# Attention kernel: the weighting of the values moved to another place in the step, on TensorE, ScalarE and VectorE

## The reference, cut to what matters

```python
# query = layernorm(x), key = value = ctx, 32 query heads, 8 key/value heads, head size 128
q = (query @ wq)   # 1024 x 4096
k = (key @ wk)     # 1024 x 1024, each head used by 4 query heads
v = (value @ wv)   # 1024 x 1024
q, k = rope(q), rope(k)
raw = einsum('bhqd,bhkd->bhqk', q, k) / sqrt(128)
attn = softmax(raw + mask, axis=-1)
out = einsum('bhqk,bhkd->bhqd', attn, v)
x = x + tanh(g) * (out.reshape(1024, 4096) @ wo)
```

## Time and profile before

| | |
|---|---|
| median of three executions | 804.2 us |
| the profiled execution | 806.3 us, of which span 804.5 us |
| TensorE (PE) busy | 762.8 us, 95% of the span |
| VectorE (DVE) busy | 640.2 us, 80% |
| ScalarE (ACT) busy | 352.2 us, 44% |
| GpSimd (POOL) busy | 388.6 us, 48% |
| mean granted TensorE clock | 0.984 |

### The profile page before, as it was taken

The page is one execution under the profiler, slowest core; times in us unless marked ns, Lnnn a source line. Parts: engine busy times, 40 slices in busy tenths (PEclk is TensorE's granted clock), DMA queues, the critical chain, the costliest instruction groups (busy, mean ns, idle before and its releaser), DMA issues.

```text
span 804.5 us, 12801 instructions
## 1 busy us (share of the span) xinstructions
PE 762.8 (95%) x4278; PEld 607.7 (76%) x4278; DVE 640.2 (80%) x1209; ACT 352.2 (44%) x1077; POOL 388.6 (48%) x352
## 2 busy tenths in 40 slices
PE   3899998898989999999999999999999999999996
PEld 2576675887767778888878888877888888787875
DVE  5999997879888787767878777787877778868985
ACT  2878884412333423343342334334333433344664
POOL 2889986415553533323353333335333333386784
PEclk9899999998999999999999999999999999999998
DMA  8310140100021111011111100111110012210011
GB/s 258 104 53 26 33 124 2 40 28 25 29 63 42 52 39 42 26 32 40 35 46 38 51 27 27 40 40 41 39 54 27 27 34 85 56 30 1 2 40 66
DMA packets 37463, 37.45 MB, mean 47 GB/s; under 512 B 2912, under 2 KB 27232, under 8 KB 37408
## 3 DMA queue, kind: packets, MB, share of 16 engines
q1 hardware_dynamic: 35488, 33.20, 13.8%
q10 hardware_dynamic: 1920, 3.54, 1.4%
HBM read 34.64 MB, written 2.10 MB: 46 GB/s over the span
## 4 chain that ended last, share of the span: by engine, by line
PE 62%; DVE 8%; POOL 5%; issue 2%; ACT 1%; POOLq 0%; DVEq 0%; ACTq 0%
PE ROW L2080 6%; PE QB L2082 6%; PE QB L2080 6%; PE QB L2081 6%; PE SB L2195 6%; PE ROW L2081 6%; PE ROW L2082 6%; PE PB L2168 4%; DVE rope_b L1695 2%; PE KV L719 2%; PE KV L2080 2%; PE TB L2138 2%; PE KV L2082 1%; PE KV L2081 1%; PE KV L720 1%
## 5 line engine op out<-in xcount | busy, mean ns | idle before, releaser
L1260 POOL TENSOR_TENSOR dense<-rope_a,rope_b 128x512 f32<-128x512 f32 x62 | 79.2, 1278 | 163.8 <-DVE rope_b L1695 163.8
L1474 ACT ACTIVATE ot_hi<-PB 128x512 fp32r<-128x512 f32 x64 | 38.3, 598 | 199.2 <-PE PB L2168 199.1
L1463 ACT ACTIVATE e_sb<-masked,nmax 128x64 f32<-128x64 f32 x256 | 86.1, 337 | 57.0 <-DVE nmax L1726 56.7
L2080 PE MATMUL QB<-xT_hi,wq_lo 128*128 128x512 f32 x256 | 106.9, 417 | 0.0
L2080 PE MATMUL ROW<-wo_hi,ot_lo 128*128 128x512 f32 x256 | 102.1, 399 | 0.8 <-DVE ot_lo L1754 0.8
L2082 PE MATMUL QB<-xT_hi,wq_hi 128*128 128x512 f32 x256 | 101.7, 397 | 0.0
L2081 PE MATMUL QB<-xT_lo,wq_hi 128*128 128x512 f32 x256 | 101.6, 397 | 0.0
L1692 DVE TENSOR_TENSOR rope_a<-QB,rope 128x512 f32<-128x512 f32 x62 | 42.8, 691 | 73.9 <-PE QB L2082 71.8
L2081 PE MATMUL ROW<-wo_lo,ot_hi 128*128 128x512 f32 x256 | 101.6, 397 | 0.0
L2082 PE MATMUL ROW<-wo_hi,ot_hi 128*128 128x512 f32 x256 | 101.1, 395 | 0.0
L1695 DVE TENSOR_TENSOR rope_b<-QB,rope 64x512 f32<-64x512 f32 x124 | 85.4, 688 | 3.9
(11 more groups left out here) (215 smaller groups left out, 1883.4 us busy)
## 6 DMA issues: line engine op xcount, KB each, us to landing
raw<-in_wq SPq DMA_DIRECT2D x32, 256.0 KB, 2.7
raw<-in_wo SPq DMA_DIRECT2D x32, 256.0 KB, 2.6
ctx_two<-in_ctx SPq DMA_DIRECT2D x16, 256.0 KB, 3.8
x_sb<-in_x SPq DMA_DIRECT2D x8, 256.0 KB, 6.8
ctx_raw<-in_ctxT ACTq DMA_DIRECT2D x1, 2048.0 KB, 12.6
raw<-in_wv SPq DMA_DIRECT2D x8, 256.0 KB, 2.7
raw<-in_wk SPq DMA_DIRECT2D x8, 256.0 KB, 2.8
out<-x_sb SPq DMA_DIRECT2D x8, 256.0 KB, 2.0
```

The costliest lines, as they stand in the source:

```text
L1260: nc.gpsimd.tensor_tensor(dst, a, b, ALU.add).then_inc(s_rot, 1)
L1463: nc.scalar.activation(e_sb[:, r, :], masked[:, r, :], ACT.Exp, bias=nmax[:, r:r + 1], accum_out=zsum[:, r:r + 1]).then_inc(s_exp, 1)
L1474: nc.scalar.activation(ot_hi[:, :, :].rearrange("p h (b q) -> p b h q", b=2), PB2[:, :, 0:256].rearrange("p b (h q) -> p b h q", h=GH), AC ...
L2080: nc.tensor.matmul(out, lhs[1], rhs[0], start=first, stop=False)
```

## The change

Two small rules are added. `behind_transposes(n)` holds for n % 4 = 0, 1, 2. `at_the_end(gp, n)` holds for n % 4 = 2 and for the last step before the fourth pair. In a step of the first kind, TensorE now issues `weighted(N-2)` between the transposes and the query; in one of the second kind, it issues `weighted(N-1)` at the old place. So n % 4 = 0 and 1 have one block, early; n % 4 = 2 has two, one early and one late; n % 4 = 3 has none. ScalarE and VectorE follow: where the block is early, ScalarE rounds `pt` (now behind a wait for that block), then `ot`, and then takes the exponentials, and VectorE takes both low parts first, then makes the probabilities, then rotates the query. The fourth pair is not changed.

```diff
+        def behind_transposes(n):
+            return n % 4 < 3
+        def at_the_end(gp, n):
+            return n % 4 == 2 or (gp, n) == (LAST - 1, SLOTS - 1)
 # ScalarE, pair()
                     if N >= 1:
+                        if N >= 2:
+                            act.wait_ge(s_pv, N - 1)
                         round_pt(N - 1)
+                    if N >= 2 and behind_transposes(n):
+                        round_ot(N - 2)
                     exps(N)
-                    if N >= 1:
+                    if at_the_end(gp, n):
                         round_ot(N - 1)
 # VectorE, pair()
-                    if N == 0:
+                    if N >= 2 and behind_transposes(n):
+                        rest_ot(N - 2)
+                    first = N == 0 or N >= 2 and behind_transposes(n)
+                    if first:
                         normalize(N)
                     if n < 12 or ahead:
                         rope_q(q_job(gp, n), N + 4, n % 4)
-                    if N:
+                    if not first:
                         normalize(N)
                     if N >= 2:
                         accumulate(N - 2, (n - 2) % 8)
-                    if N >= 1:
+                    if at_the_end(gp, n):
                         rest_ot(N - 1)
 # TensorE, pair()
                     if N >= 1:
                         transposes(N - 1)
+                    if N >= 2 and behind_transposes(n):
+                        weighted(N - 2)
...
                     if N >= 2:
                         outputs(N - 2)
-                    if N >= 1:
+                    if at_the_end(gp, n):
                         weighted(N - 1)
```

## The result

Over 14 executions each, the median is 808.8 us with the change and 804.7 us without. The ratio is 1.0050, 95% interval 1.0039 to 1.0061, so the loss is small but clear of the noise. The profiled execution took 809.42 us with a span of 807.6; before it was 806.3 with 804.5. The forecast of +3.4 us stands against +4.1 in the medians and +3.1 in the spans.

What follows compares the result with a forecast made beforehand. TensorE, busy for 95% of the span, was taken to bound the kernel. Borders 2.96, start 0.74 and neutral blocks -0.3 summed to +3.4 us: 807.6 us on the 804.2 median. Its own range was 805.2 to 810, the wider one 803.0 to 811.5.

Steps and rivals of the forecast that it cites:

- A covered block: Block lying beside a TensorE wait at the old place; moved onto TensorE's path it adds 0.74 us.
- five places: Borders at steps 4, 8, 24, 40, plus the start: +0.74 us each where a wait had covered the block.
- the start: Step 1's block, ahead of the 2.33 us wait for `p_sb`, comes behind it: +0.74 us, out of 0.7 to 1.1.
- four borders: Steps 4, 8, 24, 40, where TensorE waits for a rotated query: 4 x 0.74 = 2.96 us lost.
- The price of a block on the path: Last pair, last transpose to second matmul behind the block: 0.97 us against 0.23 without, so 0.74 us.
- The neutral blocks: The 29 early blocks where TensorE doesn't wait: -0.01 us each from a cheaper entry, -0.3 in all.
- `ot_lo` in time behind a key projection: Eleven n % 4 = 2 steps: no wait, 0.06 to 0.2 us slack; rival of late `ot_lo`: 811 us, chance 0.12.
- The slow stretch: Half clock at the start, 3.5 us, stays; rival: a second such stretch costs up to 1.7, 809.3 us, chance 0.10.
- The weights are not pulled under the transposes: Block's load starts with its matmul; rival of loads pulled ahead: 34 x -0.09 = -3.1, 804.5 us, chance 0.05.
- ScalarE and VectorE hide the new order: Step 24: exponentials from about 422.1, `p_sb` near 423.7 instead of 424.88, so the transposes don't wait.

Runs made afterwards that it cites:

- the first edit: Kernel before with VectorE's order in steps 0 to 2 alone changed, next step's mask and maximum ahead of the rotations: 802.79 us, ratio 0.9979.
- two more: On that kernel, query ahead of scores at four waiting borders: 801.59 us; then step 0's accumulation and block 1's low part ahead of query 2's rotation: 799.20 us.

## Why the prediction was right

Point by point:

- **A covered block costs its full price** (forecast 0.74 at each of five places). Shown: the experiments give 0.74 for the start and 2.98 for four borders (forecast 2.96), and the lags by step 0.70 and 3.01. The listed idle time grew as well, from 0.23 to 0.78 at the borders, just under the 0.8 to 1.0 that was forecast, and from 2.33 to 3.20 at the start; but it is not the price, since it leaves out what listed durations overlap. The choice of 0.74 for the start, out of 0.7 to 1.1 at the lower clock level, came out too.
- **The price of a block on the path**, read from the last pair, where nothing changed: 0.74, measured 0.75. The entry (the block 0.20 behind the last transpose: 420.93 against 420.61 + 0.12) and the exit (421.82 - 421.26 = 0.56, forecast 0.54) came out as well.
- **The neutral blocks** were sized at -0.3 us. The sum without them, 2.96 + 0.74 = 3.70, is nearer to the 3.84 measured, and 22 such blocks gave +0.12. The term is mis-sized: the 0.01 us by which the new entry seemed cheaper is less than the rows can tell, and such blocks cost about 0.005 each instead. From -0.3 to +0.1 is all of the 0.4 by which the sum was low.
- **`ot_lo` in time behind a key projection** (slack forecast 0.06 to 0.2; the overlap of 0.08 that it names makes the upper end 0.14). Step 22 after, VectorE and TensorE's loads, to be read against the earlier trace rows:

```profile
407.39 0.68 DVE L1766 TENSOR_TENSOR ot_lo<-PB,ot_hi 128x512 fp32r<-128x512 f32 x1
408.28 0.19 PEld L2095 LDWEIGHTS ROW<-wo_hi,ot_lo 128*128 128x128 f32 x1
```

  It ends at 408.07, 0.21 ahead of the load, or 0.15 with the handoff of 0.06. It is 0.21 in all eleven such steps (step 1 has no key projection), and no wait of ROW is listed. That rival fell, narrowly.
- **The slow stretch doesn't grow**: 3.5 us at 0.52 in both, and 0.93 in both over the whole of 216 to 240 us. Its rival fell too, though the idle time ahead of it grew as that rival said.
- **The weights are not pulled under the transposes.** TensorE's loader at the border of step 24 (idle time before it in brackets):

```profile
420.92 0.19 PEld L2183 LDWEIGHTS PB<-pt_hi,v_lo 64*128 64x128 f32 x2 [0.17 <-issue]
```

  The load starts with its matmul, after 0.17 us in which the loader did nothing, as in the earlier trace rows. The Trainium skill (TensorE: Matmul & The Clock Gate, section Step-by-step: what each phase is for) says that weight loads are pulled ahead of running matmuls if row groups don't conflict or the background buffer is the target. This load wasn't pulled ahead, so by the measurement the moved blocks gain nothing at their entry.
- **ScalarE and VectorE hide the new order**: no wait in the body for `pt_hi`, `ot_hi` or, away from the start, `p_sb`. Here the size was off on the safe side: in step 24 `p_sb` starts at 424.02, that is 8.10 behind the query's end at 415.92, where I had expected about 423.7 - 414.61 = 9.1. I had added the whole block and `round_ot`, 1.34 us, to the exponentials' start, but in the row of before ScalarE still waited for the maximum at that time; the exponentials start 0.25 later (6.42 behind the query's end against 6.17).

The range of 805.2 to 810 is wider than its terms: prices of 0.65 to 0.85 and 1.5 us for runs give 805.7 to 809.7. The median, 808.8, lies in both. What stayed open was on which side of half a per cent it would fall: the forecast of +0.4% lay just inside that bound, and the ratio came out on it.

## What to carry to other kernels

On an engine that bounds a stage, work in front of a wait is free up to the length of that wait. Before moving it, look at every wait of that engine behind the old place: where the profile lists only 0.2 us of idle time, the wait itself may be 0.9 long, since it shows only what the work in front of it leaves over. The same view read the other way finds gains: put work that is ready in front of the waits, or make the late input earlier, and then look for the next late input: the first edit moved its wait elsewhere, and it took two more until TensorE hardly waited. Compare the granted clock of the same stretch before a gain is put down to a wait. And when a rule in the code sets the order on several engines, an experiment on one engine must hold the others' orders fixed.

## What the runs showed of the hardware

I had not expected that the order of VectorE alone would change how long one of its instructions takes. The groups of `p_sb`, the multiply with both inputs in SBUF, by line (busy us and mean ns of one, idle before), before and after:

```profile
L1737 DVE TENSOR_TENSOR p_sb<-e_sb,rz 128x256 f32<-128x256 f32 x58 | 79.6, 1373 | 2.0
```

```profile
L1749 DVE TENSOR_TENSOR p_sb<-e_sb,rz 128x256 f32<-128x256 f32 x58 | 46.3, 798 | 2.0
```

The mean hides two values, and both stand in the fence of steps 23 and 24 above: 1.39 us at 418.50, beside GpSimd's add (418.34 to 419.62), and 0.43 us at 424.02. Of the 58 after, the 35 that run beside no GpSimd instruction, or for 0.02 us at most, average 0.425; before, 57 of the 58 ran beside one and averaged 1.39, and 55 of these met GpSimd's add into `dense`. Behind a rotation, `p_sb` meets the add of the same query; ahead of it, it doesn't. The Trainium skill (SBUF — State Buffer, section Who interferes with whom) says that the port pair shared by VectorE and GpSimd is an exclusive lock, and that a VectorE instruction with two SBUF inputs contends with a GpSimd instruction that reads SBUF. The trace agrees that the two disturb each other: the multiply begun 0.16 us after the add ended 0.27 after it, at 419.89. That is less than the 0.42 that it takes alone, so by the listed times it didn't stand still for the whole of the add. The group is 33.3 us shorter after, more than VectorE as a whole (28), so other groups rose by 5. In the run of VectorE's order alone VectorE lost 33 us in the same way, and that run shows that they buy nothing in this kernel, which TensorE bounds.
